# Wider attention: output added ahead of a turn, a later wait for the values, one turned copy on ScalarE, transfers after the product, fewer warm-up products

## The reference, cut to what matters

```python
q = (hidden_states @ wq).reshape(b, s, H, DK).transpose(0, 2, 1, 3)   # H, DK = 16, 64
k = ...
v = ...
scores = jnp.einsum('bhqd,bhkd->bhqk', q, k) + bias                   # bias from rel_emb, by distance
attn = softmax(scores, axis=-1)
out = jnp.einsum('bhqk,bhkd->bhqd', attn, v)
return out.transpose(0, 2, 1, 3).reshape(b, s, H * DK) @ wo           # added to x
```

## Time and profile before

| what | value |
|---|---|
| median of 3 runs | 1188.54 us (1187.53 to 1189.79) |
| the profiled execution's own time | 1187.4 us |
| its span | 1184.4 us |
| TensorE busy / VectorE / ScalarE / GpSimd | 96% / 77% / 74% / 52% |
| the wider attention in the span | about 35 to 437 us |
| granted clock of TensorE, mean | 0.999 |

### The profile page before, as it was taken

The page is one execution under the profiler, slowest core; times in us unless marked ns, Lnnn a source line. Parts: engine busy times, 40 slices in busy tenths (PEclk is TensorE's granted clock), DMA queues, the critical chain, the costliest instruction groups (busy, mean ns, idle before and its releaser), DMA issues.

```text
span 1184.4 us, 39874 instructions
## 1 busy us (share of the span) xinstructions
PE 1137.3 (96%) x15764; PEld 691.4 (58%) x15764; DVE 908.5 (77%) x2423; ACT 880.0 (74%) x2387; POOL 619.6 (52%) x406
## 2 busy tenths in 40 slices
PE   9899999999999998999999999988999899999997
PEld 3365555555655653676666666554556566666664
DVE  5788898888988978877777777757777777777763
ACT  5766676666766668887797887776869788877874
POOL 4456565665656635755465555333354455645540
PEclk9999999999999999999999999999999999999999
DMA  8422222232222322211021011011010111111110
GB/s 284 171 57 76 64 72 68 56 83 57 76 64 56 83 88 63 85 33 40 20 51 39 22 42 33 19 33 31 20 41 19 37 24 42 42 41 24 37 41 19
DMA packets 35480, 66.69 MB, mean 56 GB/s; under 512 B 6704, under 2 KB 8176, under 8 KB 35296
## 3 DMA queue, kind: packets, MB, share of 16 engines
q1 hardware_dynamic: 35296, 64.16, 20.5%
HBM read 15.32 MB, written 1.11 MB: 14 GB/s over the span
## 4 chain that ended last, share of the span: by engine, by line
PE 82%; DVE 5%; ACT 4%; issue 4%; DMA 2%; SPq 1%; POOL 1%; DVEq 0%; ACTq 0%; POOLq 0%
PE ps L311 11%; PE ps L290 10%; PE ps L1447 7%; PE ps L1410 5%; PE ps L1377 5%; PE ps L1347 5%; PE ps L1326 4%; PE ps L1316 4%; PE ps L1389 4%; PE ps L1417 4%; PE ps L1317 3%; PE ps L321 2%; PE ps L1453 2%; PE ps L274 2%; PE ps L261 2%
## 5 line engine op out<-in xcount | busy, mean ns | idle before, releaser
L242 POOL TENSOR_TENSOR arena<-arena 128x1024 f32<-128x1024 f32 x128 | 241.5, 1895 | 155.8 <-DVE arena L515 155.7
L411 ACT ACTIVATE arena<-arena 128x512 f32<-128x512 f32 x256 | 182.5, 714 | 115.1 <-DVE arena L501 115.1
L1258 POOL TENSOR_TENSOR arena<-arena 128x1024 f32<-128x1024 f32 x64 | 121.5, 1898 | 227.8 <-DVE arena L1830 227.8
L1652 ACT ACTIVATE arena<-arena 128x128 f32<-128x128 f32 x512 | 198.2, 390 | 30.1 <-DVE arena L1822 29.6
L501 DVE CUSTOM_DVE_ANT_0 arena<-ps,arena 128x512 f32<-128x512 f32 x256 | 164.4, 688 | 27.3 <-PE ps L290 24.1
L1822 DVE CUSTOM_DVE_ANT_0 arena<-ps,near,arena 128x128 f32<-128x128 f32 x512 | 144.4, 346 | 39.3 <-PE ps L1377 39.2
L511 DVE STREAM_TRANSPOSE arena<-arena 128x1024 f32<-128x1024 f32 x128 | 156.5, 1231 | 1.0 <-POOL arena L242 0.9
L311 PEld LDWEIGHTS ps<-arena 32*64 32x64 f32 x8192 | 120.2, 130 | 57.8 <-issue 32.9
L1265 POOL TENSOR_TENSOR arena<-arena 128x1024 f32<-128x1024 f32 x64 | 151.2, 2362 | 0.1
L290 PE MATMUL ps<-arena 64*128 64x512 f32 x512 | 141.9, 632 | 2.3 <-issue 0.7
L311 PE MATMUL ps<-arena 32*64 32x128 f32 x8192 | 137.5, 273 | 5.4 <-issue 3.8
(11 more groups left out here) (161 smaller groups left out, 2108.1 us busy)
## 6 DMA issues: line engine op xcount, KB each, us to landing
arena<-arena SPq DMA_DIRECT2D x191, 128.0 KB, 2.4
arena<-arena SPq DMA_DIRECT2D x64, 192.0 KB, 2.6
arena<-rel_rows SPq DMA_DIRECT2D x16, 448.0 KB, 9.2
arena<-arena SPq DMA_DIRECT2D x64, 64.0 KB, 2.1
arena<-y SPq DMA_DIRECT2D x30, 128.0 KB, 2.3
arena<-arena SPq DMA_DIRECT2D x15, 127.8 KB, 2.4
arena<-in_wqkv SPq DMA_DIRECT2D x2, 768.0 KB, 4.9
x<-in_x SPq DMA_DIRECT2D x4, 256.0 KB, 5.0
```

The source lines that it names most:

```text
L242: nc.gpsimd.tensor_tensor(e, e, scale, ALU.mult).then_inc(self.normed, 1)
L411: nc.scalar.activation(self.e[:, r % 3, i, :], self.neg[:, i, :], ACT.Exp, bias=self.nmax[:, i:i + 1], scale=-1.0, accum_out=self.sums[:, ...
L1652: nc.scalar.activation(self.e[:, s, h, :], self.neg[:, h, :], ACT.Exp, bias=self.nmax[:, h:h + 1], scale=-1.0, accum_out=self.sums[:, s, h ...
```

## The change

The warm-up products go from five and two to two and none. The values' copy 2 (turned by half, 64 partitions) is made by two activations of ScalarE, after the copy out of PSUM and a wait for it; SP makes copies 1 and 3 with four transfers, so `v_spread` rises by 64 a unit, and it waits for `o_made` of the unit two before (the end of `project_out`). `weigh(u, 0)` waits for the values' copy of its own unit at the start, and for that of unit u + 2 just ahead of the first product into bank 7. `add_out(u - 1)` moves ahead of `turn(r, 1)`.

```diff
--- before.py
+++ after.py
@@ -45,8 +45,7 @@
 LA_QK, LA_V, LA_S, LA_PT, LA_O = 2, 4, 0, 5, 7
 NEVER = 1.0e25
 TINY = 1.0e-24
-WARM = 5
-SMALL = 2
+WARM = 2
 LOG_LIMIT = 1.0e19
 AHEAD = 20 * T
 AHEAD_NORMS = AHEAD + 21 * T + 28
@@ -223,11 +222,11 @@
         for u in range(self.UNITS):
             sp.wait_ge(self.v_read, u + 1)
             if u >= 1:
-                sp.wait_ge(self.v_spread, 96 * u)
+                sp.wait_ge(self.v_spread, 64 * u)
             if u >= 2:
-                sp.wait_ge(self.weighed, u - 1)
+                sp.wait_ge(self.o_made, u - 1)
             v = self.v[:, u % 3, :, :, :].rearrange("p j t c -> p j (t c)")
-            for j in range(1, self.GROUPS):
+            for j in range(1, self.GROUPS, 2):
                 s = j * self.BLOCK
                 sp.dma_start(v[s:P, j, :], v[0:P - s, 0, :]).then_inc(self.v_spread, 16)
                 sp.dma_start(v[0:s, j, :], v[P - s:P, 0, :]).then_inc(self.v_spread, 16)
@@ -299,11 +298,13 @@
                     pe.wait_ge(self.added, u)
                 pe.wait_ge(self.q_read, min(u + 3, self.UNITS))
                 pe.wait_ge(self.k_read, min(u + 3, self.UNITS))
-                pe.wait_ge(self.v_read, min(u + 3, self.UNITS))
-                pe.wait_ge(self.v_spread, 96 * (u + 1))
+                pe.wait_ge(self.v_read, u + 1)
+                pe.wait_ge(self.v_spread, 64 * (u + 1))
                 pe.wait_ge(self.turned, 4 * (u + 1))
             for c in range(half * blocks // 2, (half + 1) * blocks // 2):
                 for a in range(self.GROUPS):
+                    if c == 0 and a == self.GROUPS - 1:
+                        pe.wait_ge(self.v_read, min(u + 3, self.UNITS))
                     rows = slice(a * self.BLOCK, (a + 1) * self.BLOCK)
                     keys = slice(c * self.BLOCK, (c + 1) * self.BLOCK)
                     for h in range(2):
@@ -399,8 +400,12 @@
             act.wait_ge(self.v_made, u + 1)
             if u >= 3:
                 act.wait_ge(self.weighed, u - 2)
-                act.wait_ge(self.v_spread, 96 * (u - 2))
-            nc.scalar.activation(self.v[:, u % 3, 0, :, :].rearrange("p a b -> p (a b)"), V, ACT.Copy).then_inc(self.v_read, 1)
+                act.wait_ge(self.v_spread, 64 * (u - 2))
+            v = self.v[:, u % 3, :, :, :].rearrange("p j t c -> p j (t c)")
+            nc.scalar.activation(v[:, 0, :], V, ACT.Copy).then_inc(self.v_read, 1)
+            act.wait_ge(self.v_read, u + 1)
+            nc.scalar.activation(v[0:P // 2, 2, :], v[P // 2:P, 0, :], ACT.Copy)
+            nc.scalar.activation(v[P // 2:P, 2, :], v[0:P // 2, 0, :], ACT.Copy)
 
         def exp(r, i):
             act.wait_ge(self.biased, 4 * r + i + 1)
@@ -543,9 +548,10 @@
             if scores and not closing:
                 turn(r, 0)
                 invert_sums(r + 1, 0)
-                turn(r, 1)
             if u >= 1:
                 add_out(u - 1)
+            if scores and not closing:
+                turn(r, 1)
             if scores:
                 add_bias(r + 1, 2)
                 add_bias(r + 1, 3)
@@ -2070,8 +2076,6 @@
                 pe.wait_ge(prepared, 2)
                 for _ in range(WARM):
                     nc.tensor.matmul(k.ps[:, 7, 0:320], k.y[:, B, 1:1 + P], k.y[:, B, 1:1 + 320], start=True, stop=True)
-                for _ in range(SMALL):
-                    nc.tensor.matmul(k.ps[:, 7, 0:1], k.y[:, B, 1:1 + P], k.y[:, B, 1:2], start=True, stop=True)
                 ahead.pe(pe)
                 t5.pe(pe)
                 local.pe(pe)
```

## The result

Before 1188.54 us (1187.25 to 1190.60), after 1181.32 us (1177.21 to 1187.05), 14 runs each: ratio 0.9941, interval 0.9929 to 0.9954. The change gains 7.2 us; I had forecast 12.4. The time lies inside the range given, but nearer to its upper end than to the forecast of 1176.1.

What follows compares the result with a forecast made beforehand. TensorE, busy 96% of the span, was taken as the bound, with stops for 256-instruction blocks. Terms -11.9 + 0.4 - 1.7 + 0.8 (transfers 0) = -12.4 us, from 1188.5 to 1176.1 us; range 1173.0 to 1183.0.

Steps and rivals of the forecast that it cites:

- The stops (-11.9): TensorE's waits for 256-instruction blocks in slow attention units: fewer warm-up products move block ends 20 deeper, removing them, -11.9 us.
- From 17 instructions in: Block ends in a weighing half: from this depth the block holds all scores, 3.8 us of work, against 3.3 to 3.9 needed.
- `add_out` and the late wait (-1.7): Ahead of `weigh`: adding the output before a turn removes 0.06 us of real wait in 29 units, -1.7 us (0 to -1.8).
- The copies (+0.8): ScalarE's two half-turned copies before the first weighing delay the square 0.3 and the exp 0.5, +0.8 us (0.2 to 1.7).
- The start (+0.4): Shorter warm-up ahead of `centre` and `vary(0)`: between -1.1 and +2.3 us depending on TensorE's clock level, taken as +0.4.
- Transfers (0): Four value transfers a unit instead of six, issued later, from the end of `project_out`; nothing on TensorE waits, 0 us.
- (a): Attention block ends: the stops stay or wander, giving 1183 if they drift, 1188.0 if they are no fetch; chance 0.14.
- (b): Late transfers run beside the instruction block transfers, each unit stands 0.5 us, slower at 1191; chance 0.04.
- (c): Start and copies cost their worst, +2.3 and +1.7, with the stops gone: 1178.9 us; chance 0.10.
- no 13 us unit: Sign of the forecast: from 60 to 410 us attention units take 11.75 us and none 13 us.
- no "issue" ahead of a score's load: Sign of the forecast: TensorE has no "issue" idle over 0.3 us ahead of a weight load of the scores.
- L522's successor: Sign of the forecast: the source line following from L522 would be gone from the waits of `weigh`.

Runs made afterwards that it cites:

- f1: Changed kernel without its transfers inside SBUF, odd value copies not made, products reading copies 0 and 2 instead: 1180.73 us, ratio 0.9941.
- e1: Kernel before with only the warm-up shortened (`WARM` 5 to 2, `SMALL` 2 to 0): 1193.91 us, ratio 1.0051.
- f3: Kernel before with `add_out` ahead of `turn(r, 1)`, the late values' wait and the short warm-up (2 and 0): 1180.92 us, ratio 0.9947.
- e2: Changed kernel with the old warm-up (`WARM` 5, `SMALL` 2) put back: 1183.67 us, ratio 0.9967.
- f2: Kernel before with only two edits, `add_out` ahead of `turn(r, 1)` and the late values' wait: 1180.36 us, ratio 0.9943.
- e3: Changed kernel with its four transfers issued at their old time, behind the end of the weighing: 1182.61 us, ratio 0.9945.
- g3: Kernel before with `add_out` moved, the late wait, ScalarE's turned copy and four transfers behind the weighing, old warm-up: 1183.72 us, ratio 0.9969.
- f4: Changed kernel with three one-column warm-up products added, block ends 12 instructions deeper: 1193.30 us, ratio 1.0039.
- g4: Kernel before with only `add_out` moved ahead of `turn(r, 1)`: 1187.39 us, ratio 1.0003.
- g1: Kernel before with `add_out` moved, the late wait and `WARM` 2, `SMALL` 5, which keeps the old block ends: 1180.97 us, ratio 0.9947.
- g2: Kernel before with `add_out` moved, the late wait and its six transfers behind the output's product: 1182.88 us, ratio 0.9958.

## Why the prediction was right, and where it was not

**Direction and forecast.** Faster, as forecast, with 7.2 us of the 12.4. That the time lies inside the range is in good part luck: the term that was to carry the gain failed, and one that I had put at 1.7 us carried it.

**The stops (-11.9).** This is the step that failed: "every block end comes 20 instructions deeper ... I expect no stop over 0.1 us". The first half held. A fp32 matmul is four instructions, the ends moved by 20, a unit stayed at 576, and the old slow units vanished. The four instructions that I took from the pattern are in the traces: beside 286 loads and 286 matmuls each unit has four wait instructions, three ahead of `weigh` and one in `score`. The second half did not: new stops of 7.5 us. I had asked only how long TensorE works between two ends and compared that with 3.3 to 3.9 us. The block beginning 33 instructions ahead of the unit passed that test easily, since it holds some 5.4 us of work (it is begun 8.0 us into a unit of 11.75, and ends 1.63 into the next). It fails because its successor is asked for not at 7.6 us of that unit, as ahead of a quick one (f1), but only when the next weighing has begun (e1, 1.26 us in; f3, 0.2 us in). The stops changed by -12.1 + 7.5 = -4.6 us in place of -11.9, and not even that is the shift's: with the old start they are 7.1 (e2). What the shift is worth depends on the rest: +6 us alone (e1), nothing that can be told with the two edits (f3 against f2), -2 to -3 in the whole change (after against e2; e3 against g3 leans the same way). The traces do not explain this last gain: the 27 units take 324.31 us in e2 and 324.72 after. "From 17 instructions in" was wrong too: at 19 (f4) the old stop is still 0.3 to 0.9 us. (Of the three stretches from an end to the next block, the one from 131.5 to 134.87 is 3.4 us, not 3.3.)

The Trainium skill (Runtime: NRT & Kernel Launch, Instruction fetch mechanics) calls crossing a block boundary "mostly hidden". By these runs it is hidden at most ends, and not at the old ends 11 in or at most of the new ones 223 in; three products of one column more make the change 12 us slower (f4).

**`add_out` and the late wait (-1.7).** The size holds for the quick units, 11.81 to 11.75. What I missed is that where the waits ahead of `weigh` are met sooner, the next block is asked for sooner (e1 against f3), which is worth far more than the 0.06 us of idle time. At the old ends that shortens the stops from 12.1 to 6.4 us (f2; 11.8 with `add_out` alone, g4), and it is what makes the shift bearable (f3 against e1). The pair of edits was the largest part of the change (7 us in f2), costed as one of the smallest.

**The copies (+0.8)**, above the upper end of 1.7 at the old start: 3.1 us (g3 against f2); at the new start nothing that can be told (e3 against f3). The instructions were sized nearly right (1.28 us for 1.1), and the two delays came to 1.3 for 0.8. What the prediction left out is the clock. In the profile after, TensorE is busy for 2.25 of the 3.69 us to 52.69, and from there to 59.52 its granted clock is 0.50; without the copies (f2, f3) the same stretch runs at 1.00. The first weighing is 2.6 us late: TensorE is 1.0 late where the exp held it (52.65 against 51.62) and 4.1 late at the last scores ahead of the weighing (60.15 against 56.09), so half the clock cost some 3.0; 1.4 of that comes back because before stood that long for a turn ahead of its first weighing. That split is worked out from the two profiles, not isolated.

**The start (+0.4).** About zero, as taken, where the copies are not there: g1, f3. `centre(0)` did run at half speed (3.85 us at 4.86), and `vary(0)`'s reader on ScalarE still came 0.7 us earlier.

**Transfers (0).** Not the cause of any stop (f1, e3). A cost of up to 2 us for six late ones is left open (g2).

**Rivals.** The time lies where (a) put it, but neither of its ways came true: no drift (the stops come at one place of the cycle from first to last) and the old ones don't stay. (b), a price of 15 us through the transfers, didn't come, and f1 leaves the transfers out of it; of (c) the start's part didn't come, the copies' part was exceeded at the old start alone. What I had listed as signs: quick units 11.75, right; no 13 us unit, wrong; no "issue" ahead of a score's load, right, as the stops moved into the weighing; L522's successor, L527, has one wait of 1.1 us in place of 30 with 24.8, right; first `weigh` 1 us later, it was 2.6.

**Still open.** What decides whether a request goes out in time. Blocks are never seen to move closer together than 3.2 us, and in f1 a second request 0.6 us late loses the third one. Over the 35 units of that kind, of the eleven whose second block moves by 4.1 us into the unit eight get the third, of the 24 later ones one does; so the time of the second decides much and not all (in e3 the third is missing although the second is on time). That the sequencer can't ask while it stands at a semaphore fits all 35 cases and the wait records (g4), but the profile shows the moving of a block and not the asking, so this last step is argued. Why the shift is worth 2 to 3 us where ScalarE's copies are there, and the copies 3 us at the old start alone, no run separates. Nor do I know why executions of the change spread over 10 us, those of f2 over 4; the profiled one, high in its range, can't tell. No kernel beat the change beyond its interval; f2 equals it with two edits. The late wait alone was not tried.

## What to carry to other kernels

Where TensorE stands for "issue" at places 256 instructions apart, look at the queue marked "instruction" and place its requests in time, not only its block ends. Short blocks are not the only ones in danger: the new stops came behind a block that holds 5.4 us of work. Here a unit was safe in all nine cases in which its block moved in the unit before, and in none of the 26 others. Ask of each wait at such a place when it is met and whether it can move to the instruction that needs it; in this kernel that was worth more than the idle time it showed. And before keeping a change made of several edits, run it without each, and in more than one company: here the shift loses 6 us by itself and gains 2 to 3 with the rest, the copy costs 3 with one start and nothing that can be told with the other, and two edits carry the whole gain.

## What the runs showed of the hardware that was not expected

- The number of one-column products at the start sets the time. In the change: none 1181.3, two 1185.4, three 1193.3 us. What each does beside its one column is to move every block end by four instructions: the stop in the first half lies behind 223, 215 and 211.
- TensorE goes on with a block only 2.3 to 2.6 us after its 16 KB have moved (e1: 1.26 to 3.58 us into the unit; f3: 0.2 to 2.76); over the 26 stops of this kind it is 2.2 to 2.9. Two blocks of it never move less than 3.2 us apart in the fourteen profiles. By these numbers a block for an end 1.63 us into a unit has to be moved by some 0.6 to 1.3 us before the unit starts (an estimate).
- TensorE's sequencer runs ahead of the engine: in f2 it comes to the waits of a weighing 4.7 us before that weighing starts. In the kernel before, where these waits are met when it passes them, each wait instruction takes 0.05 us and the next starts 0.10 to 0.11 us after the start of the one ahead of it, in all 27 turns.
- ScalarE's copy of 64 x 512 between halves of the partitions takes 0.63 us, as long as its 128 x 512 forms (0.58 to 0.60), and the next instruction starts 0.64 us later, so that nothing overlaps; a full-height one beside them is followed after 0.5 us (38.01 and 38.50 us).
- TensorE's granted clock fell from 1.00 to 0.50 (2.4 to 1.2 GHz) for 6.83 us in after (from 52.69) and g3 (from 53.40), each behind a stretch in which it was busy for 2.25 of 3.69 us and 1.96 of 3.40; in f2 it was busy for 2.30 of the 3.00 us from 49.00, and stayed at 1.00.
